# First stage written out, with two buffers in turn, the queries of its last five pairs held back, and the first cache rows fetched inside it

## The reference

```
x = x + x @ w0[cond[b]]                    # per sequence, a 64x64 matrix on the token axis
x = x + attention(x)                       # q: 8 heads, k and v: 4 heads of 64, RMS norm, rotary
                                           # new k, v written into a paged cache, window of 256 keys
x = x + x @ W2[id[b]] + b2[id[b]]          # one expert of 16 per sequence
x = x + x @ W3.T + (x @ A[ad[b]].T) @ B[ad[b]].T * scale
```

## Time and profile before

| what | value |
|---|---|
| median of 3 executions | 1178.34 us (1176.82 to 1183.21) |
| the profiled execution, own time | 1169.61 us |
| its span, first to last instruction | 1167.8 us |
| mean granted TensorE clock, share of full | 0.95 |
| PE / DVE / ACT / POOL busy | 90% / 56% / 46% / 46% |
| PE's share of the chain that ended last | 37% |
| PE waiting for cache rows (line 1233) | 49.9 us in 6 waits |

### The profile page before, as it was taken

How to read it: one execution, slowest core, us unless ns; L and a number is a source line. 1 busy time by engine, 2 the same in 40 slices (tenths; PEclk the granted TensorE clock), 3 DMA queues, 4 the chain that set the end, 5 groups by cost and what they waited for, 6 DMA issues and landing times. The chain is left out here.

```text
span 1167.8 us, 23800 instructions
## 1 busy us (share of the span) xinstructions
PE 1050.6 (90%) x6440; PEld 713.3 (61%) x6440; DVE 654.7 (56%) x1888; ACT 535.0 (46%) x1336; POOL 535.5 (46%) x597
## 2 busy tenths in 40 slices
PE   4999999999247979999999979999999999999997
PEld 2767677877124655666656646666666666666655
DVE  5889795377333535555555534555555555555552
ACT  3457765475133424544444433444444444444440
POOL 1545444245545454554454445454455554555400
PEclk9999998899666979999999989999999999999998
DMA  3343443353263646665566655656666566665640
GB/s 125 116 137 134 141 147 112 110 167 138 84 198 89 186 149 204 212 214 187 176 205 210 207 168 168 187 182 196 201 227 196 179 201 203 222 195 179 204 145 19
DMA packets 95336, 196.15 MB, mean 168 GB/s; under 512 B 31346, under 2 KB 40114, under 8 KB 87110
## 3 DMA queue, kind: packets, MB, share of 16 engines
q1 hardware_dynamic: 63942, 149.49, 37.9%
q0 software_dynamic: 30784, 44.16, 14.2%
q10 hardware_dynamic: 576, 2.10, 0.5%
HBM read 195.08 MB, written 33.56 MB: 196 GB/s over the span
## 5 line engine op out<-in xcount | busy, mean ns | idle before, releaser
L981 POOL DMA_INDIRECT KV<-kv_scratch,idxs x192 | 190.6, 993 | 290.4 <-DMA KV<-in_pool,idxs 251.4
L971 POOL DMA_INDIRECT KV<-in_pool,idxs x192 | 193.7, 1009 | 107.4 <-issue 81.8
L1130 DVE CUSTOM_DVE_ANT_0 SM<-bank,FM 128x336 f32<-128x336 f32 x256 | 129.8, 507 | 192.8 <-PE bank L1246 171.8
L1052 ACT ACTIVATE PT<-bank 112x384 f32<-112x384 f32 x256 | 111.9, 489 | 264.8 <-PE bank L1254 264.3
L1061 ACT ACTIVATE PR<-SM,nb 128x336 f32<-128x336 f32 x256 | 145.8, 577 | 0.8 <-DVE nb L1134 0.6
L1267 PE MATMUL bank<-PT,KV 112*64 112x128 f32 x1536 | 113.3, 283 | 17.3 <-ACT PT L1052 17.3
L1052 ACT ACTIVATE KT<-bank 128x336 f32<-128x336 f32 x128 | 57.6, 450 | 154.5 <-PE bank L1233 154.5
L1267 PEld LDWEIGHTS bank<-PT,KV 112*64 112x64 f32 x1536 | 86.1, 139 | 65.3 <-issue 40.5
L1292 PE MATMUL bank<-W,XT 128*64 128x512 f32 x512 | 123.7, 604 | 0.7 <-ACT XT L1052 0.7
L90 PE MATMUL bank<-wqh,XTH 128*128 128x512 f32 x256 | 108.0, 422 | 9.2 <-DVE XTL L480 8.5
L1246 PE MATMUL bank<-KT,QB 64*128 64x336 f32 x512 | 111.1, 512 | 5.6 <-ACT KT L1052 5.1
(11 more groups left out here) (157 smaller groups left out, 1934.6 us busy)
## 6 DMA issues: line engine op xcount, KB each, us to landing
W<-in_w SPq DMA_DIRECT2D x64, 1024.0 KB, 8.4
FM<-mask SPq DMA_DIRECT2D x64, 168.0 KB, 4.0
X<-in_x SPq DMA_DIRECT2D x32, 256.0 KB, 2.8
x_scratch<-X SPq DMA_DIRECT2D x32, 256.0 KB, 2.1
kv_scratch<-KVR SPq DMA_DIRECT2D x32, 256.0 KB, 2.5
qt_scratch<-QT SPq DMA_DIRECT2D x32, 256.0 KB, 2.8
QB<-qt_scratch SPq DMA_DIRECT2D x32, 256.0 KB
XB<-x_scratch SPq DMA_DIRECT2D x32, 256.0 KB
```

What stands on the lines that cost most here:

```text
L971: pool.indirect_dma_start(out=KV[k][:, c, :], out_offset=None, in_=t["pool"], in_offset=bass.IndirectOffsetOnAxis(ap=idxs[k][:, c:c + 1], ...
L981: pool.indirect_dma_start(out=KV[k][:, c, :], out_offset=None, in_=kv_d, in_offset=bass.IndirectOffsetOnAxis(ap=idxs[k][:, NCH + c:NCH + c ...
L1052: return nc.scalar.activation(dst, src, ACT.Copy)
L1130: v.tensor_tensor_reduce(out=SM[u % 2][:, :], in0=bank[u % 2][:, 0:SPAN], in1=FM[k][:, :], scale=1.0, scalar=-3e38, op0=ALU.add, op1=ALU.m ...
```

## The change

- **Written out.** `bodies` of stage one no longer makes loops: it writes out 39 bodies on every engine. The bodies now go over items: items 0 to 26 are pairs 0 to 26 in full, items 27 to 31 are keys and values alone of pairs 27 to 31, items 32 to 36 are the queries alone of pairs 27 to 31 (`HOLD` is 5).
- **Two buffers in turn** for XTH, XTL and KVR, by the item's number; the semaphore of the KVR stores is split in two. `xt(i+1)` moves on PE from behind kv(i) to in front of it.
- **Order on ACT:** the values leave bank 3 right behind the keys, and XTH(i+1) comes in front of the keys of item i.
- **Query items** need x1 again: SP loads it back from memory into X and X1 in turn (`load_back`), and PE turns it again. QR is turned two bodies later than made there.
- **First cache rows fetched in stage one:** KV[0] and KV[1] and their indices become tiles of the whole kernel; POOL issues the old rows of sequences 0 and 1 behind bodies 28 and 29 and the new rows behind bodies 32 and 34. SP loads the first queries and masks behind body 34, into the space of the raw late weights. In stage two POOL's body for pair 0 is empty and SP's first loads are gone.
- `late_low` moves from behind bodies 27, 29 to 32 to behind 27 to 31. `later` and `mr` are laid over other scratch space.

```diff
+HOLD = 5
+            FULL = PAIRS - HOLD
+            ITEMS = PAIRS + HOLD
             def bodies(eng, body, between={}):
-                cuts = sorted({1, PAIRS - 3, PAIRS - 2, PAIRS - 1, PAIRS} | set(between))
...
-                        with eng.Fori(begin, cut + 1) as p:
-                            body(p)
+                for i in range(ITEMS + 2):
+                    body(i)
+                    if i in between:
+                        between[i]()
+            def q_behind(i):
+                late = i - 2 if i >= PAIRS + 1 else i - 1
+                return late if has_q(late) and i != PAIRS + 1 else None
...
+                def body(i):                                   # DVE
+                    if has_item(i) and has_q(i):
+                        dve.wait_ge(s_qe, at(pair_of(i), 1, 0))
+                        wait(dve, s_sum, i)
+                        rotated(i, 0, H, 0, 2)
+                        wait(dve, s_qr, i)
+                        rotated(i, 0, H, 0, 1)
+                    if has_item(i + 1):
+                        turned(i + 1)
...
+                def load_back(i):                              # SP
+                    j = i - PAIRS
+                    if j == 0:
+                        sp.wait_ge(s_x1, PAIRS)
+                    elif j == 1:
+                        sp.wait_ge(s_x1o, 16 * PAIRS)
+                    if j:
+                        sp.wait_ge(s_xtp, i - 1)
+                    sp.dma_start(x1_tile(i)[:, :], x1_d[pair_of(i)]).then_inc(s_xre[j % 2], 16)
...
+                    if has_item(i - 1) and has_kv(i - 1):      # SP, body(i)
+                        sp.wait_ge(s_qr, at(i - 1, 1, 0))
+                        sp.wait_ge(s_ve, at(i - 1, 1, 0))
+                        sp.dma_start(kvd_v[bass.ds(i - 1, 1)], KVR[(i - 1) % 2][:, :]).then_inc(s_kvo[(i - 1) % 2], 16)
+                    if PAIRS < i + 2 < ITEMS:
+                        load_back(i + 2)
...
+                bodies(pool, body, {9: pages, 28: first_old(0), 29: first_old(1),
+                                    PAIRS: first_new(0), PAIRS + 2: first_new(1)})
...
+                def body(i):                                   # PE
+                    if has_item(i):
+                        pe.wait_ge(s_xt, at(i, 1, 0))
+                    if has_item(i) and has_q(i):
+                        if not has_kv(i) and has_item(i + 1):
+                            xt(i + 1)
+                        wait(pe, s_qe, pair_of(i))
...                                                            # 12 products, queries
+                    if has_item(i) and has_kv(i):
+                        xt(i + 1)
+                        wait(pe, s_ve, i)
...                                                            # 12 products, keys and values
+                    if from_x(i + 2):
+                        l0(i + 2)
...                                                            # qt(q_behind(i))
-                queries(Pair(0, 0))
-                windows(Pair(0, 0))
```

More of the change, by code:

```diff
@@ L203, in build @@
             X1 = sa("X1", [P, D])
-            XTH = sa("XTH", [P, KC, P], F32R)
-            XTL = sa("XTL", [P, KC, P], F32R)
+            XTH = [sa(f"XTH{i}", [P, KC, P], F32R) for i in range(2)]
+            XTL = [sa(f"XTL{i}", [P, KC, P], F32R) for i in range(2)]
             QK = sa("QK", [P, H + G, HD])
@@ L209, in build @@
             SW = sa("SW", [P, H + G, HD])
-            KVR = sa("KVR", [P, KVW])
+            KVR = [sa(f"KVR{i}", [P, KVW]) for i in range(2)]
             QR = sa("QR", [P, H, HD])
@@ L699, in body @@
[L699 to L704 removed]
+                    part = heads_of(i)
@@ L706, in pages, with first_new, run @@
+                def first_new(b):
+                    def run():
+                        for done in s_kvo:
+                            pool.wait_ge(done, 8 * PAIRS)
+                        pool.wait_ge(s_old[b], 16 * NCH)
+                        new_rows(pool, b)
+                    return run
                 def pages():
@@ L724, in turned @@
                     act.wait_ge(s_xtp, at(q, 1, 0))
-                    wait(act, s_kvps, q)
-                    copy(XTH[:, :, :].rearrange("p a b -> p (a b)"), bank[1][:, :]).then_inc(s_xth, 1)
+                    copy(XTH[q % 2][:, :, :].rearrange("p a b -> p (a b)"), bank[1][:, :]).then_inc(s_xth, 1)
                 for k in range(KC):
@@ L834, in body @@
                         last.then_inc(s_qps, 1)
-                        wait(pe, s_ve, p)
-                        exact_products(mm, bank[3][:, :], [(XTH[:, k, :], XTL[:, k, :], wqh[:, k, 512:1024],
+                    if has_item(i) and has_kv(i):
+                        xt(i + 1)
+                        wait(pe, s_ve, i)
+                        exact_products(mm, bank[3][:, :], [(xh[:, k, :], xl[:, k, :], wqh[:, k, 512:1024],
                                                             wql[:, k, 512:1024]) for k in range(KC)],
@@ L960, in used @@
                         return 8 * (p - 2) + 4 * (b + 1)
-                    def held(b):
+                    if isinstance(p, int) and p == 0:
+                        return
+                    for b in range(2):
                         k, n = 2 * pr.par + b, p * 2 + b
```

277 lines of the change are left out of this document (150 added, 127 removed).

## The result

| | before | after |
|---|---|---|
| median, both measured side by side (20 executions each) | 1184.38 us (1176.82 to 1204.67) | 1187.59 us (1181.53 to 1208.5) |
| ratio, 95% interval | | 1.0059 [1.0036, 1.0082] |
| the profiled execution: own time, span | 1169.61, 1167.8 us | 1185.45, 1183.6 us |
| mean granted TensorE clock | 0.95 | 0.955 |
| third sequence's index copy (start of POOL's own part of stage two) | 331.64 us | 332.52 us |

The changed kernel is 0.6% slower, at the border of what was called no change. The forecast was +4.3 us; the ratio on 1178.3 gives +7.0, with an interval of 4.2 to 9.7. The forecast median, 1182.6, lies 5.0 us under the measured one, since before too came out 6.0 us higher in these 20 executions than in its first three.

What follows compares the result with a forecast made beforehand. PE bounds the kernel nearly everywhere, POOL's fetches the start of stage two. Items 0 to 26 give -6.3 us, the stretch behind them +10.6: +4.3 on 1178.3, forecast 1182.6 us, range 1160 to 1194.

Steps and rivals of the forecast that it cites:

- Two buffers and the earlier xt: Items 0 to 26: PE's wait for XTL goes, 17 pair distances fall from 7.72 to 7.35 us, -6.3 us.
- Written out: Stage one's loops: a loop's end costs PE nothing, so writing the bodies out counts 0 us.
- Keys and values alone: Items 27 to 31: PE waits for X1, 6.3 to 6.4 us an item; 30.0 us, plus 0.8 for low clock.
- rival 4: Clock also falls in keys-and-values items, query items take 9.2 us: +12 us and more, 1190 and above; chance 0.12.
- x1 loaded back: Into the query items: xt(33) waits for pair 28's x1 from memory and starts 4.7 us after kv(31).
- Query items: Items 32 to 36: closed chain through ACT, DVE and PE, 6.6 us each, taken as 8.5 with low clock.
- rival 1: Clock holds in the query items, 6.6 us each: -6.5 us in all, 1172 us; chance 0.22.
- Tail: From the last q through QT's store to POOL's first copy in stage two: 9.7 us, against 12.0 before.
- Fetches hidden: Boundary: 22.5 us of first cache-row fetching leaves it; PE's first keys come right behind the barrier.
- rival 5: Early fetching brings nothing, KV[0] and KV[1] landing only behind the barrier: 22.5 us come back; chance under 0.02.
- Rival 2: Held items' chain is looser, near PE's content of 4.0 and 3.7 us: 1147, or 1160 halfway; chance 0.08.
- Rival 3: Stage two: one late gather less or more, about 10 us: 1172 or 1193; chances 0.13 and 0.09.

Runs made afterwards that it cites:

- e0: The changed kernel run again with no edit: ratio to before 1.0162 [1.0047, 1.0277], profiled span 1169.4 us.
- e10: The changed kernel with HOLD = 0 and all four first fetches issued behind stage one's last body: ratio to before 0.9897 [0.9848, 0.9946].
- e1: The kernel before run again with no edit: ratio 1.0012 [0.9971, 1.0053], profiled span 1166.1 us.
- e3: The changed kernel with HOLD = 0, no pair taken apart, new rows fetched behind the last pair: ratio to before 0.9735 [0.9669, 0.98].
- e9: The changed kernel with HOLD = 0 run a second time, later, beside other kernels: ratio to before 0.9831 [0.9766, 0.9897].
- e6: The changed kernel with HOLD = 2 instead of 5: ratio to before 0.9747 [0.9622, 0.9872].
- e5: The changed kernel with XTH(i+1) and XTL(i+1) in front of item i's squares and rotation, query items only: ratio to before 0.999 [0.9935, 1.0044].
- e7: The changed kernel with xt(i+1) behind kv(i) and l0(i+2) in items of keys and values alone: ratio to before 1.0109 [1.0057, 1.0161].
- e11: The changed kernel with HOLD = 8 instead of 5: ratio to before 1.0191 [1.0098, 1.0284].
- e8: The changed kernel with HOLD = 2 and the order edits of e5 and e7 together: ratio to before 0.9986 [0.9927, 1.0046].

## Why the prediction held, step by step

From the end of kv(26) to the third copy, by the profile of after:

| step | forecast | measured |
|---|---|---|
| items 0 to 26, shift of the end of kv(26) | -6.3 | 250.05 - 257.96 = -7.9 |
| keys and values alone, with the clock's share | 30.8 | about 32.6 (to 282.65) |
| wait in front of xt(33) | 4.7 | 287.20 - 282.65 = 4.5 |
| q(32) with its xt | 5.6 | 5.4 |
| the other four query items | 33.5 | 29.0 (to 321.58) |
| tail | 9.7 | 10.9 |
| sum behind kv(26) | 84.3 | 82.5 |
| shift of the third copy | +4.3 | +0.9 |

- **Two buffers and the earlier xt.** Right in direction; the 7.9 is past the bound of 7 and near the 6.3 in part by luck. By the trace of before 15 of the 26 distances are ordinary, not 17 (the next are 8.02 and 8.10). From one end of kv to the next, five of the 15 took 7.27 or 7.28 us in after, so all of PE's waiting went there; the others took 6.8 to 8.5, and the 15 together gained 3.2 us (4.7 in e0). More came from the longer distances that I had left alone: 6.1 us (5.3 in e0). Against both stands a kv(0) that ended 1.4 us later (0.5).
- **Written out.** Worth nothing that shows: 0.9955 [0.99, 1.0009], and 7.71 us in both forms. The Trainium skill, page "Runtime: NRT & Kernel Launch", section Instruction fetch mechanics, names a stall only for a taken branch whose target lies outside the fetched pages. No run shows whether the loops' branches are of that kind, so the missing price says nothing against the page, and the prediction drew too much from it.
- **Keys and values alone.** The chain was read rightly (6.2 against 6.3 to 6.4), the clock was mis-sized: two of the items ran eight and seven of their twelve products at the lower level and took 1.6 us more each, where I had 0.8 for all. In e0 one did (7.79 beside 6.20 and 6.22). That is a part of rival 4, whose condition, two of four losing the level, was met in after; its query items of 9.2 and its +12 us were not.
- **x1 loaded back.** 4.7 forecast, a wait of 4.39 measured, 5.31 in the second execution.
- **Query items.** The chain was right (6.57 with the clock kept), the level less bad than "others mostly": 8.74, 7.86, then 6.94, and five of the last item's products at the lower level again. The truth lies between the forecast (8.5) and rival 1 (6.6), and changes between executions: 9.24, 8.12, 6.92 in the second.
- **Tail.** 1.2 us longer than forecast; PE waits 3.21 us for the last QR and then 3.58 at the barrier.
- **Fetches hidden.** Right: old rows at 269 and 277 us, new rows at 299 and 316, PE's first keys right behind the barrier; rival 5 is out. The early old rows are worth 9 to 12 us by themselves (e10); what the new rows bring inside stage one, no run shows alone.
- **Rival 2** (a loose chain) is out by the distances. **Rival 3**, one late gather more or less at about 10 us, is real, as the table of long pairs shows, and is spread over all kernels.
- **The third copy as the measure.** Stage two was to be as much earlier or later as that copy is. From the copy to the end the fourteen executions took 821.6 to 858.3 us, so for one execution the measure can miss by 15 to 22 us; before, e1, e3, e9, e6 and e5 lie within 5 us of each other.

The time came out right, within a few us, and in part by luck, with errors of both signs: the third copy moved by +0.9 and +0.4 us instead of +4.3, while the executions side by side show +0.4 to +0.8% (and +0.5 to +2.8% in the second session). What makes the changed kernel some 3 to 9 us dearer than that copy's place says stays open. In e0 stage two took 839.8 us behind the copy, 2.8 to 3.6 more than in the two of before: 5 more up to the first output, 2 less in the 31 distances. More late gathers in the changed kernel would do it, but only two of its executions have a profile, one of these is the one with the stalls of ACT, and e7 and e11 ran the same stage two in 821.6 and 828.9 us.

## What to carry to other kernels

Hiding a start-up behind the stage before it is worth what the work needed to make room for it doesn't cost: here the fetches fitted into engines that stood idle anyway, and taking five pairs apart moved the third copy some 23 us back, for room that `HOLD = 0` did without, though PE stands 12.4 us at its barrier (with `HOLD = 2` the best kernel here, 2 to 3% faster than before). When a body is split into two thinner ones, write down for each the chain through *all* engines and the place of each step in its queue: what was covered by the other half's products becomes the period. And before moving a transpose or a load past a wait, ask which load is issued behind it, as the order of keys and values showed.

## What the runs showed of the hardware

- Gaps of 2.06, 1.52, 1.78 and 1.96 us between l0 and xt were followed by products at 0.43 us from start to start behind the first and the third, and at 0.23 behind the other two (items of 7.80, 6.21 and 7.79 us, same execution). Behind the wait for x1 loaded back the clock had fallen at 3.75 (e7), 3.85 (e8), 4.03 (e5), 4.39, 5.31 and 6.32 us (e6), and had not at 3.81 (e11): the length of the wait alone does not decide it.
- The time of an execution grows in steps with its late gathers: 746.9 us for stage two's 31 distances with no long pair, 755 to 757 with one, 765 to 771 with two, 778.5 with three, 788.8 with four. From the third copy to the end that is 821.6 to 858.3 us, more than most edits here are worth. These are different kernels; executions of one kernel also differ by some 30 us (1154.29 to 1185.96 for before in one session), but few of them have a profile, so that late gathers are the whole of it is not shown.
- In one execution of fourteen ACT stood thirteen times, 20.3 us in all, in front of its copies, with a releaser that the profile can't name. Its 31 distances came to 776.2 us, 29 above the execution without a long pair; the stalls did not come back.
